# Four rows of x to a partition, pairs of batches in four staggered 32x128 array tiles, and the last two units in eight 32x64 tiles

## What is computed

```python
B, C, D, T, N_SUBJECTS = (128, 64, 64, 512, 8)
x = x + einsum('bct,bcd->bdt', x, L0_cond_weights[itok_B_0_7])      # 8 x 64 x 64
x = x + einsum('bct,bcd->bdt', x, L1_cond_weights[itok_B_1_198])    # 200 x 64 x 64
return x
```

## Time and profile before

| | before |
|---|---|
| median of 3 runs (lowest to highest) | 92.88 us (92.76 to 93.39) |
| the profiled execution: its own time | 92.78 us |
| the profiled execution: span from first to last instruction | 91.0 us |
| TensorE busy / weight loads busy | 78.5 us (86%) / 44.7 us (49%) |
| VectorE / ScalarE / GpSimd busy | 61.8 / 58.6 / 23.4 us |
| moved by DMA | 35.93 MB, mean 395 GB/s over the span |

### The profile page before, as it was taken

The page is one execution under the profiler, slowest core; times in us unless marked ns, Lnnn a source line. Parts: engine busy times, 40 slices in busy tenths (PEclk is TensorE's granted clock), DMA queues, the critical chain, the costliest instruction groups (busy, mean ns, idle before and its releaser), DMA issues.

```text
span 91.0 us, 2427 instructions
## 1 busy us (share of the span) xinstructions
PE 78.5 (86%) x890; PEld 44.7 (49%) x890; DVE 61.8 (68%) x127; ACT 58.6 (64%) x117; POOL 23.4 (26%) x119
## 2 busy tenths in 40 slices
PE   0499939994999999999999999999999999999200
PEld 0389929983554544364454445445454544444000
DVE  1087008995288888796887878788777888778700
ACT  2899806886276767585777667677666777577500
POOL 3400029999999959300000000000000000000000
PEclk9999999999999999999999999999999999999995
DMA  0999989999999999999999999999999999999993
GB/s 9 334 411 421 461 342 427 412 412 407 411 411 402 412 400 414 409 421 420 418 418 414 423 420 418 416 418 421 423 407 423 418 418 421 421 414 376 414 420 140
DMA packets 9181, 35.93 MB, mean 395 GB/s; under 512 B 721, under 2 KB 850, under 8 KB 9042
## 3 DMA queue, kind: packets, MB, share of 16 engines
q1 hardware_dynamic: 4512, 16.78, 46.3%
q10 hardware_dynamic: 4514, 16.91, 45.8%
q0 software_dynamic: 144, 2.10, 5.4%
HBM read 19.01 MB, written 16.78 MB: 393 GB/s over the span
## 4 chain that ended last, share of the span: by engine, by line
PE 70%; DMA 13%; DVE 9%; issue 1%; DVEq 1%; ACTq 0%; POOLq 0%
PE psum L219 62%; DMA w_rows<-in_L_cond_weights_dram,cond 10%; DVE w L238 7%; PE psum L200 7%; DMA subjects<-in_itok_B_dram 2%; DVEq L69 1%; DVE xy L260 1%; PE psum L180 1%; DVE m_diag L252 1%; ACTq L318 0%; DVE w_rows L313 0%; POOLq L149 0%; DVEq L244 0%
## 5 line engine op out<-in xcount | busy, mean ns | idle before, releaser
L219 PE MATMUL psum<-xy,m_diag 64*128 64x512 f32 x256 | 57.1, 596 | 0.5 <-DVE m_diag L252 0.5
L260 DVE COPY xy<-psum 64x512 f32<-64x512 f32 x64 | 43.7, 683 | 13.2 <-PE psum L219 12.2
L260 ACT COPY xy<-psum 64x512 f32<-64x512 f32 x64 | 37.2, 581 | 19.8 <-PE psum L219 19.0
L219 PEld LDWEIGHTS psum<-xy,m_diag 64*128 64x128 f32 x256 | 24.8, 187 | 27.1 <-issue 25.7
L157 POOL COPY w0b<-w0t 64x64 f32 x112 | 21.6, 235 | 11.0 <-DMA w_rows<-in_L_cond_weights_dram,cond 8.5
L200 PEld LDWEIGHTS psum<-w,w0b 64*32 64x32 f32 x512 | 5.6, 105 | 6.4 <-issue 3.8
L238 ACT COPY w<-psum 64x256 f32<-64x256 f32 x16 | 5.8, 364 | 4.1 <-PE psum L180 3.1
L180 PE MATMUL psum<-ident,w_rows 128*64 128x128 f32 x64 | 7.2, 274 | 1.4 <-DVE w_rows L313 1.4
L252 DVE TENSOR_SCALAR m_diag<-psum,mask 128x256 f32<-128x256 f32 (+1 forms) x18 | 7.3, 449 | 1.1 <-PE psum L200 0.9
L326 ACT COPY w<-w_rows 128x256 f32<-128x256 f32 x18 | 7.3, 405 | 0.9 <-DMA w_rows<-in_L_cond_weights_dram 0.3
L180 PEld LDWEIGHTS psum<-ident,w_rows 128*64 128x64 f32 x64 | 7.0, 152 | 1.6 <-DVE w_rows L313 1.6
(11 more groups left out here) (8 smaller groups left out, 2.3 us busy)
## 6 DMA issues: line engine op xcount, KB each, us to landing
xy<-in_x_dram SPq DMA_DIRECT2D x15, 1024.0 KB, 19.0
out_dram<-xy ACTq DMA_DIRECT2D x15, 1024.0 KB, 11.0
xy<-in_x_dram SPq DMA_DIRECT2D x2, 512.0 KB, 5.9
out_dram<-xy ACTq DMA_DIRECT2D x2, 512.0 KB, 4.3
w_rows<-in_L_cond_weights_dram ACTq DMA_DIRECT2D x1, 128.0 KB, 2.6
cond<-in_itok_B_dram SPq DMA_DIRECT2D x1, 0.5 KB, 2.4
subjects<-in_itok_B_dram ACTq DMA_DIRECT2D x1, 0.5 KB
w_rows<-in_L_cond_weights_dram,cond POOLq DMA_INDIRECT x1, 9.5
```

The costliest lines, as they stand in the source:

```text
L219: last = nc.tensor.matmul(psum[:, 2 * (s % Y_RING) + h, :], m_diag[rows, odd, v % M_RING, j, :], xy[rows, s, j * T:(j + 1) * T], start=j = ...
L260: copy(xy[rows, s, i * T:(i + 1) * T], psum[HALVES[i], 2 * (s % Y_RING) + h, :]).then_inc(done, 1)
```

## The change

x of units 0 to 13 is loaded with four neighbouring rows to a partition (8 KB that lie together), 16 partitions to a batch, so that 32 partitions hold a pair of batches and a unit is four pairs. `xy` gets two more slots, and y of unit v is written where x of unit v-1 stood (output still has 32 partitions to a batch and two rows to each, so stores of these units are as before).

`products(k)` now always makes two units: the row halves of the array are the two units of the block, and each of its 32 matmuls multiplies W0 rows of a pair of batches with W1 of both, 128 columns in place of 64; `copy_m` keeps the blocks that belong together by the mask (made from the identity by one reduction) and drops the crossed ones. VectorE copies M of the even unit, ScalarE that of the odd one.

`apply(v, half, j)` does one row j of two pairs: two matmuls of 32x128 weights by 512 columns into a pair of banks. y(n) with n = 2v + half collects four j. The two halves of a unit run one j apart: half 0's j beside half 1's j-1, so that four array tiles are in use. `USES` is the order in which four pairs of banks go round over M and y, and the order in which both copying engines work. products(k+1) stands ahead of the odd unit of block k.

The last two units (`LAST` = 14) are loaded with two rows to a partition in four DMAs of 512 KB; their M is copied without mask to `m_last`, and a half of a unit takes eight matmuls on 32x64 tiles. Their output is two batches by 64 channels, copied in one 128x512 copy for each engine, and stored by SyncE in four DMAs of 512 KB with 2 KB rows, each when its two copies are done. `w0t_last` is a second form of W0 for them, made by VectorE after its early copies.

The diff, cut to its core (left out are constants, tensor shapes and semaphores, GpSimd's old loop, the mask, and the view in `copy_w1`, which now counts batches as eight to a unit):

```diff
+    assert ROWS == J
+    M_RING = 4
+    TWOS = 4
+    USES = [("m", 0)]
+    for k in range(BLOCKS):
+        USES += [("y", 4 * k), ("y", 4 * k + 1)]
+        if k + 1 < BLOCKS:
+            USES += [("m", k + 1)]
+        USES += [("y", 4 * k + 2), ("y", 4 * k + 3)]
...
-    x_view = x_dram.rearrange("(s b) (p j) t -> (b p) s (j t)", b=SLOT, j=J)
-    out_view = out_dram.rearrange("(s b) (q i) t -> (b q) s (i t)", b=SLOT, i=J)
+    QUARTERS = [slice(r * H, (r + 1) * H) for r in range(PAIRS)]
+    x_view = x_dram.rearrange("(v b) (p j) t -> (b p) v (j t)", b=UNIT, j=J)
+    last_x_view = x_dram.rearrange("(v r o) (p i) t -> v o r p (i t)", r=PAIRS, o=2, i=I)
+    out_view = out_dram.rearrange("(s b) (q i) t -> (b q) s (i t)", b=UNIT // 2, i=I)
+    last_out_view = out_dram.rearrange("(n o) c t -> (o c) n t", o=2)
...
+        def bank(kind, n):
+            return 2 * (USES.index((kind, n)) % TWOS)
+        def x_of(v):
+            return xy[:, 2 * v + 2:2 * v + 4, :].rearrange("q s t -> q (s t)")
...
         def _(sp):
-            def load(s, n):
-                sp.dma_start(xy[:, s:s + n, :], x_view[:, s:s + n, :]).then_inc(s_x[s // 2], 16)
             sp.dma_start(cond[:, :], cond_dram.rearrange("(b o) -> b o", o=1)).then_inc(s_cond, 16)
-            load(0, 2)
-            load(2, 1)
-            sp.wait_ge(s_w0b_early, EARLY * UNIT)
-            load(3, 1)
-            for v in range(2, UNITS):
-                load(2 * v, 2)
+            sp.dma_start(x_of(0), x_view[:, 0, :]).then_inc(s_x[0], 16)
+            for j in range(0, J, 2):
+                sp.dma_start(x_of(1)[:, j * T:(j + 2) * T], x_view[:, 1, j * T:(j + 2) * T]).then_inc(s_x[1], 16)
+                if j == 0:
+                    sp.wait_ge(s_w0b_early, BLOCK * UNIT)
+            for v in range(2, LAST):
+                sp.dma_start(x_of(v), x_view[:, v, :]).then_inc(s_x[v], 16)
+            for v in range(LAST, UNITS):
+                for o in range(2):
+                    sp.dma_start(xy[:, 2 * v + 2 + o, :], last_x_view[v, o]).then_inc(s_x[v], 16)
+            for n in range(2 * LAST, 2 * UNITS):
+                sp.wait_ge(s_y_v, 2 * (n + 1))
+                sp.wait_ge(s_y_s, 2 * (n + 1))
+                sp.dma_start(last_out_view[:, 2 * n:2 * n + 2, :],
+                             xy[:, n, :].rearrange("q (r t) -> q r t", r=2)).then_inc(s_out[n // 2], 16)
             for v in range(UNITS):
-                sp.wait_ge(s_out[v], 32 if v == UNITS - 1 else 16)
+                sp.wait_ge(s_out[v], 32 if v >= LAST else 16)
+        def put_w0(eng, done, picked, v, n):
+            rows = HALVES[v % 2]
+            if v >= LAST:
+                eng.tensor_copy(w0b[rows, v // 2, n * C:(n + 1) * C],
+                                w0t_last[rows, bass.ds(picked * C, C)]).then_inc(done, 1)
+            else:
+                eng.tensor_copy(w0b[rows, v // 2, :].rearrange("q (r j b p) -> q r b j p", r=PAIRS, j=J, b=2)
+                                [:, n // 2, n % 2, :, :],
+                                w0t[rows, bass.ds(picked * C, C)].rearrange("q (j p) -> q j p", j=J)
+                                ).then_inc(done, 1)
...
+                    pool.wait_ge(s_w0t, 2)
+                if first == LAST:
+                    pool.wait_ge(s_w0t_last, 2 * I)
+                for n in range(BLOCK * UNIT):
+                    put_w0(nc.gpsimd, s_w0b, picked[n], first + n // UNIT, n % UNIT)
...
             def products(k):
-                first, n = BLOCKS[k]
-                if first + n <= EARLY:
-                    pe.wait_ge(s_w0b_early, UNIT * (first + n))
+                if k == 0:
+                    pe.wait_ge(s_w0b_early, BLOCK * UNIT)
                 else:
-                    pe.wait_ge(s_w0b, UNIT * (first + n - EARLY))
-                if k >= 2:
-                    pe.wait_ge(s_m_v, 2 * k)
-                    pe.wait_ge(s_m_s, 2 * k)
-                for v in range(first, first + n):
+                    pe.wait_ge(s_w0b, k * BLOCK * UNIT)
+                wait_for_banks("m", k)
+                if BLOCK * k == LAST:
+                    for o in range(2):
+                        for j in range(I):
+                            for r in range(PAIRS):
+                                for odd, rows in enumerate(HALVES):
+                                    at = (o * I + j) * C
+                                    n = 2 * r + o
+                                    last = nc.tensor.matmul(psum[QUARTERS[r], bank("m", k) + odd, at:at + C],
+                                                            w0b[rows, k, n * C + j * H:n * C + (j + 1) * H],
+                                                            w1[rows, k * UNIT + n, :], start=True, stop=True)
+                else:
                     for j in range(J):
-                        for r in range(SLOT):
+                        for r in range(PAIRS):
                             for odd, rows in enumerate(HALVES):
-                                at = (v % M_COLUMNS * J + j) * C
-                                last = nc.tensor.matmul(psum[QUARTERS[r], M_BANKS[k] + odd, at:at + C],
-                                                        w0b[rows, v * SLOT + r, j * Q:(j + 1) * Q],
-                                                        w1[rows, v * SLOT + r, :], start=True, stop=True)
+                                at = (r * J + j) * 2 * Q
+                                n = k * UNIT + 2 * r
+                                last = nc.tensor.matmul(psum[QUARTERS[r], bank("m", k) + odd, j * P:(j + 1) * P],
+                                                        w0b[rows, k, at:at + 2 * Q],
+                                                        w1[rows, n:n + 2, :].rearrange("q b e -> q (b e)"),
+                                                        start=True, stop=True)
                 last.then_inc(s_m_psum, 1)
-            def apply(k):
-                first, n = BLOCKS[k]
-                pe.wait_ge(s_m_v, 2 * (k + 1))
-                pe.wait_ge(s_m_s, 2 * (k + 1))
-                for s in range(2 * first, 2 * (first + n)):
-                    v, odd = s // 2, s % 2
-                    pe.wait_ge(s_x[v], 32 if v == 1 else 16)
-                    if s >= Y_RING:
-                        pe.wait_ge(s_y_v, 2 * (s - Y_RING + 1))
-                        pe.wait_ge(s_y_s, 2 * (s - Y_RING + 1))
-                    for j in range(J):
-                        for h, rows in enumerate(HALVES):
-                            last = nc.tensor.matmul(psum[:, 2 * (s % Y_RING) + h, :],
-                                                    m_diag[rows, odd, v % M_RING, j, :],
-                                                    xy[rows, s, j * T:(j + 1) * T],
-                                                    start=j == 0, stop=j == J - 1)
+            def wait_for_m(v):
+                pe.wait_ge(s_m_v, 2 * (v // BLOCK + 1))
+                pe.wait_ge(s_m_s, 2 * (v // BLOCK + 1))
+            def apply(v, half, j):
+                n = 2 * v + half
+                if j == 0:
+                    wait_for_banks("y", n)
+                for h in range(2):
+                    rows = QUARTERS[2 * half + h]
+                    last = nc.tensor.matmul(psum[:, bank("y", n) + h, :], m_diag[rows, v % M_RING, j, :],
+                                            xy[rows, 2 * v + 2 + j // 2, j % 2 * T:(j % 2 + 1) * T],
+                                            start=j == 0, stop=j == J - 1)
+                if j == J - 1:
                     last.then_inc(s_y_psum, 1)
+            def apply_last(v, half):
+                n = 2 * v + half
+                wait_for_banks("y", n)
+                for j in range(I):
+                    for h in range(2):
+                        rows = QUARTERS[2 * half + h]
+                        for o, columns in enumerate(HALVES):
+                            last = nc.tensor.matmul(psum[columns, bank("y", n) + h, :], m_last[rows, v - LAST, o, j, :],
+                                                    xy[rows, 2 * v + 2 + o, j * T:(j + 1) * T],
+                                                    start=j == 0, stop=j == I - 1)
+                last.then_inc(s_y_psum, 1)
             pe.wait_ge(s_w1_v, TURNS)
             pe.wait_ge(s_w1_s, TURNS)
             products(0)
-            for k in range(len(BLOCKS)):
-                if k + 1 < len(BLOCKS):
-                    products(k + 1)
-                apply(k)
+            for v in range(LAST):
+                if v % BLOCK == 1:
+                    products(v // BLOCK + 1)
+                wait_for_m(v)
+                pe.wait_ge(s_x[v], 32 if v == 1 else 16)
+                for j in range(J):
+                    apply(v, 0, j)
+                    if j > 0:
+                        apply(v, 1, j - 1)
+                    elif v > 0:
+                        apply(v - 1, 1, J - 1)
+            apply(LAST - 1, 1, J - 1)
+            for v in range(LAST, UNITS):
```

(137 more changed lines are left out.)

25 lines of the change are left out of this document (18 added, 7 removed).

## The result

The changed kernel takes 107.03 us (median of 6 runs, 106.92 to 107.14) against 92.88 us (92.54 to 93.39): ratio 1.152, 95% interval 1.149 to 1.155. It is slower, as forecast, but by 14.2 us and not by 3.1: 107.0 lies outside the range of 91.8 to 98.8.

What follows compares the result with a forecast made beforehand. TensorE and DMA both looked full, TensorE barely in time. Unit 13's end: 77.88 + 0.77 + 0.86 + 7 x (0.21 + 0.10) = 81.68 us; stores then land 3.2 us later: 92.78 + 3.2 = 96.0 us, range 91.8 to 98.8.

Steps and rivals of the forecast that it cites:

- Work that is covered: Step on VectorE's `w0t_last` and mask, GpSimd's copies, `copy_w1` and SyncE's loads: all hidden, no cost added.
- SyncE's load order and its one wait stay: Claim on SyncE's queue, priced at nothing; its four late stores stand behind loads issued long before.
- stretch sum: Stores at the end: unit 11 lands at 81.1 us, unit 12 at 85.8, the last four at 93.7 against 90.5.
- Its signs: Profile checks: four weight loads every 0.43 us, products 1.07 us, block 8.2 us, DMA below full about 77 to 82 us.
- dry stretch behind unit 11: DMA queue runs dry behind unit 10's store; unit 11 lands at 81.1 us, unit 12, issued at 80.9, at 85.8.
- Insertion: Products put between apply work on TensorE: 128 columns add 0.21 us to each of seven (bounds 0.1 and 0.43).
- Wait for M: TensorE stalls because VectorE copies y(4k+1) ahead of the next block's M: 0.1 us a block (bounds 0 and 0.4).
- Loads with 8 KB: Loads of 14 units: one 8 KB packet takes 304 ns against 313 for two of 4 KB, 0.9 us less DMA work.
- 2 KB stores: The last stores, 2.1 MB in 2 KB packets: 82 in place of 78 ns each, 5.0 us becomes 5.3.
- four row tiles do not run at full rate: Rival on apply's 32x128 tiles: 145 us if two at a time, 132 if weight loads go singly; chance 0.11.
- DMA sets the end: Rival: DMA stays full and absorbs TensorE's lateness, so faster, 92.0 us (91.4 with loads at 437 GB/s); chance 0.10.
- the start: Before the first apply: products(0) makes both units and copies are larger, so apply starts at 23.39, not 22.62, +0.77 us.
- the stagger: Unit halves on TensorE run one round apart: 57 rounds in place of 56, +0.86 us, and stores are issued later.

Runs made afterwards that it cites:

- spread loads: Changed kernel with each of the four loads of the last two units cut into four of 32 partitions: 97.35 us, ratio 1.047.
- run at 64 columns: Changed kernel with those four loads cut into four of 32 partitions, and products of units 0 to 13 at 64 columns, not 128: 95.54 us.
- kernel before with four: Kernel before with only its last two units' loads changed to four of 512 KB, HBM side 4 by 32 rows of 4 KB: 108.26 us.

## Why the prediction was wrong, point by point

- **The step that failed** is "Work that is covered", with "SyncE's load order and its one wait stay", and with it the stretch sum, which took every transfer at 419 GB/s over 16 engines. The four last loads were priced as bytes in 4 KB rows; how their HBM side is cut was not looked at. The runs showed that they hold a quarter of the DMA engines, and that the transfers left on these end late: 9.7 us of the 14.2. The Trainium skill, DMA: Bandwidth & Descriptors, Why a DMA increments its semaphore by 16 and not by 1, says that a DMA uses the largest number of engines up to 16 that divides the slowest dimension of both sides. The runs agree: an HBM side of 4 leaves 25.7% of the engines at work near the end and takes 108.3 us, one of 8 leaves 51.1% and takes 97.6, and loads of 32 partitions at a time give back 9.7. It was not weighed in the prediction.
- **The direction was right, for less than a third of the loss.** "Slower" was forecast for TensorE's lateness and the late stores behind it, and these bear on the 4.5 us that remain with spread loads. The larger part of the loss has a cause that the forecast did not have. Its signs do not tell the two apart: weight loads came four at a time, a block took 8.30 us, DMA fell below full, and still the time lay far outside. No sign looked at when the last loads land.
- **The rest of the sum held, in part by luck.** Without the four loads' fault the time is 97.35 us, forecast 96.0. Unit 13 ends at 82.55 (81.68): apply starts 0.35 later than reckoned, a block takes 8.30 in place of 8.17 us. TensorE's end, 86.18 us against 86.1, is luck: unit 13 is 0.9 late, but the last two units take 3.64 us and not 4.3. The dry stretch behind unit 11 is there, 1.7 us long, and the store of unit 12 lands after 4.4 us (4.9).
- **Insertion**: +0.21 us forecast; 1.09 for 0.79 in the chain is +0.30, inside its bounds. Only six of the seven insertions are longer: the seventh makes M of the last two units with 64 columns and still takes 0.79. The run at 64 columns shows the weight of the others.
- **Wait for M**: +0.1 forecast; apply of a block takes 7.21 against 7.07, +0.14. In the changed kernel the weight loads stand idle once in a block, for M, as here:

```profile
57.23 0.31 PEld L282 LDWEIGHTS psum<-xy,m_diag 32*128 32x128 f32 x8 [0.68 <-DVE m_diag L345]
```

- **Loads with 8 KB**: 0.9 us less DMA work forecast; the rate rose by 2.4% (2.7% forecast), and in the kernel before the time fell by 0.5.
- **2 KB stores**: 82 ns a packet and 400 GB/s forecast. In the run with spread loads 88 to 92 us moved 379 GB/s, so the four stores take 0.3 us more than reckoned:

```profile
DMA packets 766, 1.52 MB, mean 379 GB/s; under 512 B 47, under 2 KB 47, under 8 KB 766
q1 hardware_dynamic: 729, 1.43, 96.7%
```

- **Rivals**: "four row tiles do not run at full rate" would have given a time near this one, but for a reason that the trace refutes: four weight loads every 0.43 us, 64 records in 7.21 us. "DMA sets the end" is true of the result, but not as that rival had it: a quarter of the engines does, and the kernel is slower.
- **What stays open**: of the 4.5 us left, 1.8 are products' columns (part of it is the start, 0.2 us earlier in that run), and perhaps 0.8 the late stores. The start (1.1 us by the chain), the stagger and the wait for M were not taken out one by one, and these parts need not add up.

## What to carry to other kernels

Price a DMA by the engines that it runs on, not by its bytes alone: look at the outermost dimension of both sides after merging. In these runs 4 meant a quarter of the engines and 8 half of them; one DMA for each 32 partitions removed the loss. A DMA row that stands at a fixed low share at the end of a page (2 tenths, or 4 to 5) can be the sign of a transfer on a few engines, even if that one was issued 40 us earlier: in the changed kernel the tail was stores, after the loads had landed. Where TensorE and DMA are both full, a gain on one (8 KB rows, faster last tiles) counts only as far as the other follows.

## What the runs showed of the hardware

- Loads of 512 KB with 4 KB rows whose HBM side is 4 by 32 hold a quarter of the DMA engines: 25.7% of 16 with the stores that share them, at 105 GB/s in all (kernel before with four). With 8 by 16 the tail of stores stands at 51.1% and 210 GB/s. In the changed kernel stores of 1 MB then take 18.6 us to land (median), 11.0 before.
- After TensorE has waited 14.3 us for x, 16 records take 6.67 us at a mean granted clock of 0.55 (kernel before with four), where 16 took 3.71 in the kernel before.
- Four float32 tiles of 32x128 run as fast as two of 64x128: the weight loads of a step come every 0.43 us in both.
- 8 KB load packets move 423 GB/s against 413 for 4 KB; stores with 2 KB packets 379 over 128 partitions, and 346 in pieces of 64 partitions.
